# Four layers on one core: TensorE multiplies the identity by itself in the first layer and in the second feed-forward

## What is computed

```
x = x + L0_xattn(layernorm(x), ctx)     # quantised product q1 @ q2, no softmax
x = x + L0_ffn(layernorm(x))            # weight looked up from 4-bit codes, x @ W.T + bias
x = x + L1_xattn(layernorm(x), ctx)     # 16 heads over latent keys
x = x + L1_ffn(layernorm(x))            # int4 activations, ternary gate/up, relu^2, int8, ternary down
x = x + L2_xattn(layernorm(x), ctx)     # 32 heads, 8 groups
x = x + L2_ffn(...) ; L3_xattn ; L3_ffn # the tail
```

## Time and profile before

| what | value |
|---|---|
| median of 3 runs | 959.06 us (956.89 to 959.95) |
| the profiled execution's own time | 955.02 us |
| its span, first to last instruction | 953.3 us |
| mean granted TensorE clock over the span | 0.939 of full speed |
| TensorE matmuls busy | 797.9 us (84%) |
| VectorE busy | 732.6 us (77%) |
| ScalarE busy | 526.6 us (55%) |
| GpSimd busy | 454.2 us (48%) |
| stretch of the first layer's block | 0 to 84 us |
| stretch of `layer1_ffn` | 218.7 to 281.2 us |

### The profile page before, as it was taken

One profiled execution on the slowest core, in us unless ns is written; L12 is line 12 of the kernel. 1 busy time (PEld: TensorE's weight loads), 2 busy tenths in 40 slices (PEclk: granted clock), 3 DMA queues, 4 the chain that ended last, 5 costly groups with the idle time before them and its releaser, 6 DMA issues. The chain is left out here.

```text
span 953.3 us, 16477 instructions
## 1 busy us (share of the span) xinstructions
PE 797.9 (84%) x5138; PEld 646.2 (68%) x5142; DVE 732.6 (77%) x1710; ACT 526.6 (55%) x1419; POOL 454.2 (48%) x395
## 2 busy tenths in 40 slices
PE   0676776884488889999999999999999998788478
PEld 0264455662247678889889889988898897653156
DVE  8685587777872889788788788797887888639964
ACT  6564476884333665755675666657657656421230
POOL 4741488002912375584573755745845746343010
PEclk9778899997799999999999999999999999998879
DMA  8414365008111022031120210220210301030001
GB/s 316 137 62 146 125 221 186 6 1 284 49 29 61 1 89 69 1 115 39 49 83 22 88 55 11 88 66 0 88 66 24 108 22 66 23 98 10 1 0 45
DMA packets 38057, 70.32 MB, mean 74 GB/s; under 512 B 5697, under 2 KB 15489, under 8 KB 37890
## 3 DMA queue, kind: packets, MB, share of 16 engines
q1 hardware_dynamic: 38018, 69.83, 22.1%
HBM read 64.48 MB, written 5.34 MB: 73 GB/s over the span
## 5 line engine op out<-in xcount | busy, mean ns | idle before, releaser
L2063 DVE TENSOR_SCALAR_CACHE_REDUCE xn<-ctxT,candidate 128x512 bf16<-128x512 f32 x248 | 174.4, 741 | 0.0
L1808 ACT ACTIVATE layer_attention_probs<-xnT,stats 128x512 f32<-128x512 f32 x128 | 94.1, 736 | 130.5 <-DVE stats L1913 130.5
L1603 PE MATMUL bank<-layer_attention_keysT,layer_attention_queriesT 128*128 128x512 f32 x384 | 122.2, 427 | 3.2 <-DVE layer_attention_queriesT L1906 3.1
L1925 DVE TENSOR_TENSOR layer_attention_probsT<-bank,layer_attention_probsT 128x512 fp32r<-128x512 f32 x128 | 88.2, 689 | 46.2 <-ACT layer_attention_probsT L1816 44.7
L1603 PEld LDWEIGHTS bank<-layer_attention_probsT,layer_attention_values 128*128 128x128 f32 x768 | 98.9, 190 | 14.7 <-issue 5.2
L1603 PE MATMUL bank<-layer_attention_probsT,layer_attention_values 128*128 128x256 f32 x768 | 102.5, 283 | 6.1 <-DVE layer_attention_probsT L1925 5.5
L1603 PE MATMUL bank<-layer_attention_wo,layer_attention_headsT 128*128 128x512 f32 x384 | 102.2, 409 | 2.9 <-issue 2.9
L1816 ACT CAST layer_attention_probsT<-bank 128x512 fp32r<-128x512 f32 x128 | 74.7, 584 | 51.2 <-PE bank L1676 51.2
L1603 PE MATMUL bank<-layer_attention_l_wkv,layer_attention_l_ctxT 128*128 128x256 f32 x768 | 99.5, 283 | 1.5 <-PEq L1131 1.5
L1603 PEld LDWEIGHTS bank<-layer_attention_l_wkv,layer_attention_l_ctxT 128*128 128x128 f32 x768 | 97.0, 191 | 4.5 <-issue 2.0
L1603 PE MATMUL bank<-layer_attention_l_wq,layer_attention_xnT 128*128 128x512 f32 x384 | 93.3, 392 | 0.0
(11 more groups left out here) (306 smaller groups left out, 1723.7 us busy)
## 6 DMA issues: line engine op xcount, KB each, us to landing
layer_attention_l_raw_qo<-in_wqT SPq DMA_DIRECT2D x9, 1024.0 KB, 5.0
xnT<-inverse_sums SPq DMA_DIRECT2D x16, 512.0 KB, 3.7
layer_attention_l_raw_qo<-in_woT SPq DMA_DIRECT2D x8, 1024.0 KB, 7.0
tw_raw<-in_w_gateT SPq DMA_DIRECT2D x8, 688.0 KB, 4.9
tw_raw<-in_w_upT SPq DMA_DIRECT2D x8, 688.0 KB, 4.2
tw_raw<-in_w_downT SPq DMA_DIRECT2D x6, 768.0 KB, 4.7
layer_attention_l_raw_kv<-in_wkvT SPq DMA_DIRECT2D x9, 512.0 KB, 5.0
ternary<-tw_rounded SPq DMA_DIRECT2D x8, 344.0 KB, 2.5
```

What stands on the lines that cost most here:

```text
L1603: last = pe.matmul(out, stationary[f][a], moving[f][b], start=f == 0 and x == 0, stop=f == count - 1 and x == 2)
L1808: a.activation(probs[:, u % 3, :], masked[:, u % 2, :], ACT.Exp, bias=negmax[:, u:u + 1], scale=-1.0, accum_out=sums[:, u:u + 1]).then_inc ...
L1925: v.tensor_tensor(probsT[:, 1, p % 2, :, columns], T[u % 2][:, :].rearrange("p (c q) -> p c q", c=CPB), probsT[:, 0, p % 2, :, columns], A ...
L2063: own(k.nc.vector.tensor_scalar(k.flags[:, r % 2], row_tile(k.ctxT, r), k.candidate[:, r:r + 1].bitcast(F32), 0.0, ALU.is_ge, ALU.add, acc ...
```

## The change

A helper issues `count` matmuls of the 16-bit identity (128 x 128) by itself, repeated four times side by side (512 columns), into a whole bank. Nothing reads the result. It is called at five places of `layer0` (10, 16, 6, 4 and 12 matmuls) and at two of `layer1_ffn`: 28 before `turn4(0)`, and 10 at the head of each `turn8(t)` but the first. That is 48 and 58 matmuls. At three places a wait is added ahead of it, so that the bank is no longer being read.

```diff
+def keep_busy(k, bank, count):
+    for _ in range(count):
+        k.nc.tensor.matmul(bank[:, :], k.ident16[:, :], k.ident16[:, :].unsqueeze(1).broadcast_to([P, KT, P]),
+                           start=True, stop=True)
...
                 turn_weight(0)
+                keep_busy(k, WT[1], 10)
                 add_bias()
+                keep_busy(k, WT[1], 16)
                 pe.wait_ge(S_["cols_ready"], B)
...
                 feed_forward(0)
+                keep_busy(k, WT[1], 6)
                 turn_weight(1)
                 feed_forward(1)
+                pe.wait_ge(S_["weightT_ready"], 1)
+                keep_busy(k, WT[0], 4)
                 turn_weight(2)
                 feed_forward(2)
+                pe.wait_ge(S_["weightT_ready"], 2)
+                keep_busy(k, WT[1], 12)
                 turn_weight(3)
                 feed_forward(3)
...
+                keep_busy(k, T[0], 28)
                 turn4(0)
                 turn4(1)
...
                 def turn8(t):
+                    if t:
+                        pe.wait_ge(x8T_ready, 2 * (t - 1) + 1)
+                        keep_busy(k, T[0], 10)
                     pe.wait_ge(x8_ready, t + 1)
```

## The result

The changed kernel takes 964.29 us (median of 12 runs, 960.27 to 969.10), the kernel before 958.77 us (median of 12). The ratio is 1.0057, with a 95% interval of 1.0041 to 1.0073: slower by 5.5 us. The profiled execution took 964.73 us, its span is 963.0 us. Its mean granted clock is 0.946, against 0.939 before: the clock rose, and the kernel got slower.

The account below looks back on a forecast made before the run. The prediction took a first-layer chain through all engines, set by turn_weight(1), and TensorE without large waits after 262.7 us as bounds. First layer -1.35 plus tens +6.5 gave +5.1 on 959.06: 964.2 us, range 957.0 to 969.0.

Parts of the forecast that it names:

- The price of an added matmul: One 16-bit 128x128 by 512-column matmul on TensorE: 0.216 us at full clock, 0.42 us at the lower level.
- The tens: 30 matmuls before turn8(1), turn8(2) and turn8(3): no wait covers them, +6.5 us, bounds 4.3 and 8.6.
- The 28 at the entry: Before turn4(0): 7.5 us inside an empty 8.2; gate_up(0) 1.3 us sooner, but nothing gained overall, bounds 0 and 8.5.
- GpSimd's hold: Second feed-forward, tile 1: VectorE's L1239 stands while GpSimd's L1399 runs, so arriving 1.3 us sooner means waiting 1.3 longer.
- rival C: Second feed-forward: gains at the entry, in tile 0 and from the avoided stall total 8.5 us; -3.4 us overall, chance 0.12.
- Rivals B and C: Second feed-forward: VectorE's tile 1 rounding passes ahead of GpSimd's L1399; B +0.6 us, chance 0.25; C -3.4 us, chance 0.12.
- `turn_weight(3)` and `feed_forward(3)`: First layer: at full clock they fall from 1.12 to 0.60 and 5.97 to 3.84 us, -2.65 us, bounds -2.65 and 0.
- rival D: Clock not held around turn_weight(3), so the 2.65 us gain stays away; first ten of turn8 slow; +9.9 us, chance 0.16.
- The matmuls around the bias: First layer, 10 before and 16 behind the bias: hidden by waits and ScalarE's leaves, cost 0 and gain 0.
- The six: Before turn_weight(1) in the first layer: all on the critical chain with no wait, +1.3 us, bounds 0 and 2.5.
- the chain named above: First layer: turn_weight(1), GpSimd's and ScalarE's leaves, VectorE's 9.47 us pick, TensorE's 4.87 us wait; turn_weight(1) sets the end.
- The rule on transposes: Transposes don't count for the clock gate: gate_up(0) would start slow, sum still +5.1 us, rivals gaining at the entry void.

Follow-up runs that it names:

- e2: The kernel before with only the 10 added matmuls ahead of each turn8 but the first; 964.06 us, ratio 1.0048.
- f2: f1 with GpSimd's L1399 issued as four instructions of a quarter; 958.03 us, ratio 1.0016 to the kernel before.
- e1: The changed kernel without the 10 added matmuls ahead of each turn8; 958.98 us, ratio 1.0005 to the kernel before.
- e3: The kernel before with the 48 added matmuls of the first layer alone; 959.27 us, ratio 1.0014.
- f1: The change without the six before turn_weight(1) and the tens, but 16 and 24 ahead of the third chunks of gate_up(1), gate_up(2); 957.77 us, ratio 1.0000.
- e4: The kernel before with the 28 added matmuls at the start of the feed-forward alone; 958.80 us, ratio 1.0012.
- f3: The kernel before with 112 transposes of the 16-bit identity at the start of the feed-forward; 953.54 us, profiled once.
- f4: The kernel before with 28 one-row matmuls at the start of the feed-forward; 957.71 us, profiled once.
- g2: The change without six, four and tens, plus 16 before third-tile transposes, 6 after turn4, 22 and 34 before third chunks of gate_up(1), gate_up(2); 957.50 us, ratio 0.9981.

## Why the prediction was right, and where its steps were not

- **The price of an added matmul** (0.216 us) held: 2.16 us for ten.
- **The tens** (+6.5 us, no cover) are the loss: `turn8(3)` is 6.4 us later, the kernel without them is level with the kernel before, and they alone cost 0.48% (0.23 to 0.73).
- **The 28 at the entry** ended in time, 0.65 us before VectorE's rows came, and `gate_up(0)` ran at the full clock (4.84 us). The gain vanished at GpSimd's hold, as forecast, though in VectorE's third instruction, not the second. Two details of this step were off. GpSimd's instruction did move: it began 1.1 us later, at 251.56, partly because a copy ahead of it was held by VectorE (2.54 us in place of 1.89). And tile 0's rounding gave 1.2 us, which the prediction had only in rival C; the hold took that too. Rivals B and C did not occur: every profile in which L1399 was whole has a held VectorE instruction in tile 1 (4.37 us in e2, 5.05 to 5.07 in the others), and with L1399 cut, in f2, the gain went elsewhere.
- **`turn_weight(3)` and `feed_forward(3)`**: the gain was forecast at 2.65 us and is 0.47 + 2.13 = 2.6 in the profiled execution. The waits around `turn_weight(3)`, 0.80 and 0.68 us, did not lose the clock, the risk that rival D named.
- **The matmuls around the bias** cost and gained nothing that shows, and `feed_forward(0)` began slow again, both as forecast.
- **The six** were mis-sized. The step reads "All six are on the chain named above: +1.3 us". `turn_weight(1)` did come 1.55 us later (0.5 of it the later start of this execution), but `turn_weight(3)` only 0.93 later, so 0.4 us is what they cost. The chain was misread in one link: VectorE's 9.47 us in the earlier trace rows were not all its own work (the same three copies of block 2 take 4.54 us in the changed kernel) but to a large part the hold by GpSimd's L764. The cut of that instruction shows it. GpSimd's leaves, which before met VectorE's copies (3.63 us), ran alone when late (3.03), and that gave 0.6 us back.
- **Layer 1 gave back** what the first layer gained, a step that the prediction lacked. It said that the next block starts sooner by the whole sum. The block did start 1.66 us sooner (83.04 against 84.70), but ScalarE's copies of the normed rows only 0.85 (94.52 against 95.37). They stand behind sums of weight pieces, and SyncE issues those pieces only as ScalarE gets through the earlier ones, which stand behind `turn_weight(3)`: 79.03 us in place of 78.56.

```profile
83.64 1.48 ACT L324 ACTIVATE tw_raw<-tw_raw 128x1536 f32<-128x1536 f32 x1 [3.30 <-DMA tw_raw<-in_w_downT]
...
86.36 1.48 ACT L324 ACTIVATE tw_raw<-tw_raw 128x1536 f32<-128x1536 f32 x1 [1.14 <-DMA tw_raw<-in_w_downT]
```

  In B, the five kernels that carried the whole set of 48 in the first layer, or all of it but the six (the change, e1, e3, f1, f2), lie at 142.9 to 145.4 us, the five without any added matmul in the first layer (before, e2, e4, f3, f4) at 141.2 to 142.8. How much of that is this wait and how much the clock's ups and downs in layer 1's attention was not separated. In the profiled execution of the change, 1.2 of the 1.8 us had come by the first turned probabilities (30.26 us from the keys, against 29.09); the rest lies behind them, where the granted clock from 112 to 130 us was 0.80, against 0.99 before.
- The forecast of 5.1 us against 5.5 measured is thus partly luck: in the profiles the six cost 0.9 less than said, and layer 1 gave back 0.8 us that the sum lacked.
- **The rule on transposes** would not have changed the sum. In the Trainium skill, TensorE: Matmul & The Clock Gate, Part 4 (PE-mode transpose), it is that they do not count as activity for the clock gate. The run with 112 transposes disagrees: the granted clock went from 0.50 to 1.00 with nothing else on TensorE. The measurement decides.

## What to carry to other kernels

Work added to keep TensorE's clock up is free only where a wait ends later than it does: look at the row of the instruction behind it, and if that shows no idle time before the edit, every added matmul is paid in full. Fill waits, not gaps between busy groups, and leave little of them open: in the first layer the clock held for `feed_forward(3)` with 0.8 to 1.4 us open behind the twelve, and was lost with 1.7 us or more. A higher mean clock is not the aim; here it rose from 0.939 to 0.946 with a loss of 5.5 us.

Before paying for a faster producer, look for what holds its consumer. Here two long GpSimd instructions swallowed what a faster TensorE gained. Cutting the one in the first layer, on top of the added matmuls, gave 2.5 us by the medians; cutting the one in the feed-forward gave nothing, as the work slid onto the next tile. So a cut, too, has to be followed to the block's end.

## What the runs showed of the hardware

- The granted clock rose from 0.50 to 1.00 under nothing but transposes: 0.50 from 217 to 220 us, 1.00 from 220.2 us on (one execution, f3_transposes).
- It fell to 0.50 under one-row matmuls that kept TensorE busy without a break for 10.6 us, and stayed there (one execution, f4_one_row). Matmuls with 128 rows, started at the full clock behind the same wait of 2.10 us, kept it (6.20 us for 28, in f1, f2 and g2).
- A VectorE instruction of 0.88 us took 5.06 us beside one GpSimd instruction of 5.0 us, and 1.83 us beside quarters of it. The two took turns: VectorE's instruction ended 0.74 us after the quarter that GpSimd was in, and the next quarter 1.12 us after VectorE's. The same held between predicated copies and GpSimd's split of 6.6 us in the first layer. The Trainium skill, SBUF — State Buffer, Who interferes with whom, says that a VectorE instruction in a two-port mode, or with two inputs in SBUF beside a GpSimd instruction that reads it, contends for a shared pair of ports, and that whoever has the pair keeps it for the whole instruction while the other blocks. The rows agree, though none shows which mode VectorE's instructions were in, and the cut instructions show that the length of the holder's instruction sets the price.
